# A software-pipelined attention and ternary kernel: the order of TensorE's steady step laid out anew

## What is computed

```python
q    = x + embed[stage][..., None]          # one value per row
attn = softmax(einsum('bsd,btd->bst', q, f))
y    = einsum('bst,btd->bsd', attn, f)
xh   = y @ H                                # 256x256 Hadamard
scale = clip(max|xh|, 1e-5) / 7
xq   = clip(round(xh / scale), -8, 7) * scale
wq   = ternary(weight)                      # -1, 0, 1 times a scale of each row
out  = x + einsum('bsi,oi->bso', xq, wq)
```

## Time and profile before

| | |
|---|---|
| three runs | 111.09, 111.1 and 112.66 us, median 111.1 |
| span of the profiled execution | 111.0 us (its own time lies within 0.1 us of the median, so little lies around the span) |
| busy share of the span | PE 93%, PEld 87%, DVE 80%, ACT 66%, POOL 39% |
| period of a steady step | 5.86 us, 12 steps |
| granted TensorE clock | full, except in the last two of the page's 40 slices (from 105.5 us), where it is half |

### The profile page before, as it was taken

One profiled execution on the slowest core, in us unless ns is written; L12 is line 12 of the kernel. 1 busy time (PEld: TensorE's weight loads), 2 busy tenths in 40 slices (PEclk: granted clock), 3 DMA queues, 4 the chain that ended last, 5 costly groups with the idle time before them and its releaser, 6 DMA issues.

```text
span 111.0 us, 2674 instructions
## 1 busy us (share of the span) xinstructions
PE 103.2 (93%) x853; PEld 96.2 (87%) x853; DVE 88.6 (80%) x217; ACT 73.5 (66%) x185; POOL 43.2 (39%) x50
## 2 busy tenths in 40 slices
PE   5999999999999999999999999999999999997360
PEld 2579899899999999999999999999999999996220
DVE  0165689799898988888898979797989898989681
ACT  5045885858787777777777778695878777494410
POOL 4025799304341461336243434343434031227150
PEclk9999999999999999999999999999999999999955
DMA  3986341405253352606161526252530202020214
GB/s 86 277 306 199 102 166 37 158 0 184 106 145 145 81 202 40 241 26 235 34 224 55 189 94 189 94 189 94 158 125 0 94 0 97 0 94 0 94 41 148
DMA packets 7630, 13.19 MB, mean 119 GB/s; under 512 B 834, under 2 KB 1608, under 8 KB 7624
## 3 DMA queue, kind: packets, MB, share of 16 engines
q1 hardware_dynamic: 7612, 13.12, 35.8%
q10 hardware_dynamic: 12, 0.00, 0.0%
HBM read 8.92 MB, written 4.19 MB: 118 GB/s over the span
## 4 chain that ended last, share of the span: by engine, by line
PE 84%; DVE 8%; ACT 3%; issue 2%
PE score_bank L415 18%; PE xh_bank L415 18%; PE fh_bank L415 14%; PE f_bank L404 6%; PE prob_bank L404 6%; PE out_bank L415 6%; PE q_bank L404 6%; PE out_bank L372 4%; PE code_bank L404 3%; DVE raw_scale L704 2%; DVE abs_max L697 1%; ACT prob L598 1%; PE score_bank L382 1%; ACT code L570 1%; DVE abs_max L822 1%
## 5 line engine op out<-in xcount | busy, mean ns | idle before, releaser
L304 POOL TENSOR_TENSOR result<-scaled,x_all 128x512 f32<-128x512 f32 x13 | 16.8, 1291 | 35.7 <-DVE scaled L714 35.7
L295 POOL TENSOR_TENSOR q_nat<-x_all,bias 128x512 f32 (+1 forms) x15 | 15.6, 1042 | 20.9 <-DMA x_all<-x_dram 15.2
L561 ACT CAST f_hi<-f_bank 128x512 fp32r<-128x512 f32 x16 | 9.4, 587 | 13.9 <-PE f_bank L404 13.9
L728 DVE TENSOR_TENSOR fh_lo<-fh_bank,fh_hi 128x512 fp32r<-128x512 f32 x16 | 11.0, 690 | 5.9 <-ACT fh_hi L592 5.9
L598 ACT ACTIVATE prob<-score_bank,neg_max 128x256 f32<-128x256 f32 x32 | 15.0, 479 | 0.8 <-DVE neg_max L755 0.8
L570 ACT ACTIVATE code<-xh_bank,inv_scale 128x256 f32<-128x256 f32 x30 | 12.8, 486 | 3.6 <-DVE inv_scale L709 3.6
L415 PE MATMUL fh_bank<-had,f_hi 128*128 128x256 f32 x64 | 14.4, 307 | 0.0
L415 PE MATMUL score_bank<-f_hi,q_hi 128*128 128x256 f32 x64 | 14.1, 301 | 0.0
L592 ACT CAST fh_hi<-fh_bank 128x512 fp32r<-128x512 f32 x16 | 9.4, 588 | 6.3 <-PE fh_bank L415 6.3
L415 PE MATMUL fh_bank<-had,f_lo 128*128 128x256 f32 x64 | 13.0, 284 | 0.0
L415 PE MATMUL score_bank<-f_lo,q_hi 128*128 128x256 f32 x64 | 12.9, 283 | 0.0
(11 more groups left out here) (99 smaller groups left out, 232.8 us busy)
## 6 DMA issues: line engine op xcount, KB each, us to landing
f_nat<-f_dram SPq DMA_DIRECT2D x16, 256.0 KB, 2.7
x_all<-x_dram SPq DMA_DIRECT2D x16, 256.0 KB, 2.8
out_dram<-result SPq DMA_DIRECT2D x14, 256.0 KB, 2.0
had_raw<-hadamard_dram SPq DMA_DIRECT2D x1, 256.0 KB, 3.2
w_raw<-weight_dram SPq DMA_DIRECT2D x1, 256.0 KB, 4.8
out_dram<-result SPq DMA_DIRECT2D x2, 128.0 KB, 1.7
out_dram<-scaled SPq DMA_DIRECT2D x1, 256.0 KB, 2.0
stage_of<-itok_dram ACTq DMA_DIRECT2D x1, 0.4 KB
```

The costliest lines, as they stand in the source:

```text
L295: nc.gpsimd.tensor_tensor(q_nat[:, b.k], x_all[:, b.at].rearrange("p (t d) -> p t d", t=T), bias[:, b.at].unsqueeze(2).broadcast_to([P, T, ...
L304: nc.gpsimd.tensor_tensor(result[:, b.k], as_rows(scaled[:, b.k]), x_all[:, b.at], ALU.add).then_inc(result_ready, 1)
L561: nc.scalar.copy(f_hi[:, b.k], f_bank[:, :, :]).then_inc(f_hi_ready, 1)
L728: return nc.vector.tensor_tensor(low, of[:, :, :], high.bitcast(F32), ALU.subtract)
```

## The change

Nothing is computed otherwise; the order is new. On PE a steady step is now written as three mixed blocks. `turns_with_score`: each of the four transposes of `prob` (batch i-2) stands ahead of one fp32r matmul of `score` (i-1), and eight more of these follow. `ternary_with_hadamard`: four fp32r matmuls of `times_hadamard`, the four code transposes (i-3), and then the four ternary matmuls, now of batch i-4 in place of i-3, each ahead of one of the other four Hadamard matmuls. `turns_with_mix`: the transposes of f and q, now of batch i+1 in place of i, each ahead of one of the first eight matmuls of `mix` (i-2); four more follow. ACT's list begins with `quantize` and ends with the splits of f and q of batch i+1; the exponentials come before `decode` and `split_fh`. DVE's list has `neg_max` directly behind `f_lo`, and `scaled` moves from behind `out_scale` to behind the sums. Step 3 is written out, with the transposes of batch 4 added and without a ternary product, and `times_ternary` of batch 12 stands ahead of the tail. POOL and SP are not touched.

```diff
+            def turns_with_score(b_prob, b_score):
+                wait(pe, prob_ready, b_prob.at + 1)
+                wait(pe, prob_lo_ready, b_prob.at)
+                wait(pe, f_lo_ready, b_score.at + 1)
+                wait(pe, q_lo_ready, b_score.at + 1)
+                wait(pe, prob_ready, b_score.at)
+                for n in range(6 * T):
+                    if n < C * T:
+                        turned = turn_one(prob_bank, prob, ident[:, :], n)
+                        if n == C * T - 1:
+                            turned.then_inc(prob_in_bank, 1)
+                    mm = product_one(score_bank, scored(b_score), n)
+                mm.then_inc(score_in_bank, 1)
+
+            def ternary_with_hadamard(b_code, b_out, b_fh):
+                parts = [(f_hi[:, b_fh.k], had), (f_lo[:, b_fh.k], had)]
+                wait(pe, f_lo_ready, b_fh.at + 1)
+                wait(pe, fh_lo_ready, b_fh.at)
+                for n in range(2 * C):
+                    mm = product_one(fh_bank, parts, n)
+                turn_code(b_code)
+                if b_out:
+                    wait(pe, code_t_ready, b_out.at + 1)
+                    wait(pe, scaled_ready, b_out.at)
+                for n in range(2 * C):
+                    if b_out:
+                        mm = product_one(out_bank, [(code_t[:, b_out.k], tern_t)], n)
+                        if n == T * C - 1:
+                            mm.then_inc(out_in_bank, 1)
+                    mm = product_one(fh_bank, parts, 2 * C + n)
+                mm.then_inc(fh_in_bank, 1)
+
+            def turns_with_mix(b_load, b_mix):
+                if b_load:
+                    wait(pe, f_loaded[b_load.k], 16 * b_load.half + 16)
+                    wait(pe, f_lo_ready, b_load.at)
+                wait(pe, prob_hi_ready, b_mix.at + 1)
+                wait(pe, fh_lo_ready, b_mix.at + 1)
+                wait(pe, code_ready, b_mix.at)
+                for n in range(6 * T):
+                    if n == 2 * C:
+                        if b_load:
+                            wait(pe, q_ready, b_load.at + 1)
+                            wait(pe, q_lo_ready, b_load.at)
+                        wait(pe, prob_lo_ready, b_mix.at + 1)
+                    if b_load and n < C * T:
+                        turned = turn_one(f_bank, f_nat[:, b_load.k], ident[:, :], n)
+                        ...
+                    elif b_load and n < 2 * C * T:
+                        turned = turn_one(q_bank, q_nat[:, b_load.k], ident[:, :], n - C * T)
+                        ...
+                    mm = product_one(xh_bank, mixed(b_mix), n)
+                mm.then_inc(xh_in_bank, 1)
             def step(batch):
...
+                turns_with_score(batch(LAG_MIX), batch(LAG_SCORE))
+                ternary_with_hadamard(batch(LAG_QUANT), batch(LAG_OUT), batch(LAG_SCORE))
+                turns_with_mix(batch(LAG_LOAD_TURN - 1), batch(LAG_MIX))
...
 # ACT
-                (split_f, LAG_LOAD_TURN), (split_q, LAG_LOAD_TURN), (quantize, LAG_QUANT),
-                (split_prob, LAG_MIX), (decode, LAG_QUANT), (split_fh, LAG_SCORE),
-                (exponentials, LAG_SCORE))
+                (quantize, LAG_QUANT), (split_prob, LAG_MIX), (exponentials, LAG_SCORE),
+                (decode, LAG_QUANT), (split_fh, LAG_SCORE),
+                (split_f, LAG_LOAD_TURN - 1), (split_q, LAG_LOAD_TURN - 1))
...
 # DVE
-                (scales, LAG_QUANT), (scale_out, LAG_OUT), (split_f, LAG_LOAD_TURN),
+                (scales, LAG_QUANT), (split_f, LAG_LOAD_TURN), (maximum, LAG_SCORE),
                 (split_q, LAG_LOAD_TURN), (split_prob, LAG_MIX), (sums, LAG_MIX),
-                (maximum, LAG_SCORE), (split_fh, LAG_SCORE))
+                (scale_out, LAG_OUT), (split_fh, LAG_SCORE))
```

More of the change, by code:

```diff
@@ L405, in turn, with turn_one, product_one @@
                 return mm
+            def turn_one(to, of, by, n):
+                c, t = divmod(n, T)
+                return pe.transpose(to[:, c, t * P:(t + 1) * P], of[:, t, c * P:(c + 1) * P], by)
+            def product_one(to, parts, n):
+                t, k = divmod(n, len(parts) * C)
+                (left, right), c = parts[k // C], k % C
+                return pe.matmul(to[:, t], left[:, c, t * P:(t + 1) * P], right[:, c],
+                                 start=k == 0, stop=k == len(parts) * C - 1)
             def product(to, parts, tiles=range(T), wait_for_last_part=None):
@@ L438, in score @@
                 wait(pe, prob_ready, b.at)
-                product(score_bank, [(q_hi[:, b.k], f_hi[:, b.k]), (q_hi[:, b.k], f_lo[:, b.k]),
-                                     (q_lo[:, b.k], f_hi[:, b.k])]).then_inc(score_in_bank, 1)
+                product(score_bank, scored(b)).then_inc(score_in_bank, 1)
             def low_half_words(of):
@@ L502, in _ @@
             mix(b0)
[L503 to L510, removed]
+            b3, b4 = Batch(0, 3), Batch(0, 4)
+            turn_f(b3)
+            turn_q(b3)
+            turn_prob(b1)
+            score(b2)
+            turn_code(b0)
+            weights()
+            times_hadamard(b2)
+            turn_f(b4)
+            turn_q(b4)
+            mix(b1)
+            pe.wait_ge(tern_t_ready, 1)
+            pe.wait_ge(row_ready, 1)
             for i in range(4, 2 * LOOP_FROM):
                 step(peeled(i))
-            with pe.Fori(LOOP_FROM, B // 2) as half:
+            with pe.Fori(LOOP_FROM, B // 2 - 1) as half:
                 for odd in range(2):
                     step(looped(half, odd))
-            third_last, second_last, last = (Batch(0, B - n) for n in (3, 2, 1))
+            for i in range(B - 2, B):
+                step(peeled(i))
+            fourth_last, third_last, second_last, last = (Batch(0, B - n) for n in (4, 3, 2, 1))
+            times_ternary(fourth_last)
             score(last)
@@ L611, in step @@
                         stage(b)
-            b0, b1, b2, b3 = (Batch(0, n) for n in range(4))
+            b0, b1, b2, b3, b4 = (Batch(0, n) for n in range(5))
             split_f(b0)
@@ L641, in _ @@
             decode(b0)
+            exponentials(b2)
             split_fh(b2)
-            exponentials(b2)
+            split_f(b4)
+            split_q(b4)
             for i in range(4, 2 * LOOP_FROM):
                 step(peeled(i))
-            with act.Fori(LOOP_FROM, B // 2) as half:
+            with act.Fori(LOOP_FROM, B // 2 - 1) as half:
                 for odd in range(2):
                     step(looped(half, odd))
+            for i in range(B - 2, B):
+                step(peeled(i))
             third_last, second_last, last = (Batch(0, B - n) for n in (3, 2, 1))
@@ L796, in _ @@
             split_q(b2)
[L797 to L801, removed]
+            b3 = Batch(0, 3)
+            scales(b0)
+            split_f(b3)
+            split_q(b3)
+            split_prob(b1)
+            sums(b1)
+            maximum(b2)
+            weight_copies()
+            split_fh(b2)
             for i in range(4, 2 * LOOP_FROM):
```

14 lines of the change are left out of this document (7 added, 7 removed).

## The result

The changed kernel takes 114.64 us (median of 4 executions, 114.23 to 114.94) against 111.3 us of the kernel before in the same series (111.09 to 112.66): ratio 1.029, 95% interval 1.025 to 1.033. In a second, longer series it was 1.019 (1.007 to 1.032). Their spans are 111.0 and 113.1 us, 2.1 apart. About 1.8 us of the time lies outside the span in every execution of which both are known (114.88 us for the span of 113.1).

What follows compares the result with a forecast made beforehand. PE's own instructions were taken to bound the kernel, 5.86 us a step. Ring steps, entry and step 3 sum to +2.1 us; against the median of 111.1 that gives 113.2 us, range 112.3 to 113.9, with rivals 110.6 to 115.0.

Steps and rivals of the forecast that it cites:

- The lock: On DVE, `raw_scale`, with two SBUF operands, waits until POOL's whole `q_nat` is over; predicted about 0.4 to 0.6 us.
- The ring: Loop of DVE and POOL alone through `q_nat`, `raw_scale`, `scaled`, `result`: period 6.07 us, total +2.1 us, 113.2; chance 0.60.
- Rival A: On DVE and POOL, the lock does not bite and `raw_scale` slips through: 111.0 us; chance 0.14.
- Rival C: On PE, changing kind costs up to 0.03 us at 16 places: 116.6 us, or 114.7 at 0.02; chance 0.16.
- PE's own sum: PE's instructions in a steady step after the change: 5.86 - 0.02 = 5.84 us.
- (c): On PE, a bf16 operand follows an fp32r matmul four times a step, not twice: about 0.01 each, +0.03 at most.
- (a): On PE, fp32r matmuls and transposes standing singly cost and bring nothing: 0, bounds -0.01 to +0.03 each.
- (b): At PE's code transposes, a ternary matmul with quickly loaded bf16 weights now stands behind: 0.29 falls to about 0.24, -0.05.
- the first shift of phase: One-time cost of entering the ring: about 0.1 us.
- step 3: Exponentials before `split_fh` on ACT make fh_lo of batch 2 later and push the first steady `abs_max`: 0.1 us.
- The tail: End of the run: the one moved ternary product only stands ahead of existing waits: 0, at most 0.2 us.

Runs made afterwards that it cites:

- `ternary_by_code`: Kernel before, with only the ternary matmuls (batch i-4) in one block directly behind the code transposes and `scaled` behind the maximum on DVE: ratio 1.007 (1.001 to 1.013).

## Why the prediction was right, and where it was not

**The lock and its place.** The mechanism was right: `q_nat` directly behind `result`, the wait for x gone from the steady steps, `raw_scale` ending with `q_nat` in ten steps, PEld waiting some 0.2 us for ACT's `code`. Only the size of the sign was off: `raw_scale` of 0.27 to 0.40 us, for the most part 0.35 to 0.38, where the text had 0.4 to 0.6. Two edits that leave POOL's work alone in amount (one moves it, one changes the operands' place) take the lengthening of `raw_scale` away.

**The ring.** Worked out as 6.07 us in POOL's loop; the six steps from 43.34 to 79.86 are 6.09. With one link of 0.13 out, it gave back 0.10; with PE made faster or later it didn't move. The eleven steady steps cost +1.99, where the prediction had 1.9 for ten of them. Of the cases, the ring (0.60) came in. Rival A is out, since the lock bites in every one of these steps. Rival C has the right sign, at 0.006 a change in place of 0.02 to 0.03.

**PE's own sum.** The wrong sign, and a small error. Predicted 5.84; with the ring gone the kernel runs at 5.88 in the steps where nothing waits. The term that failed most is (c), "about 0.01 each time, +0.03 at most": the four ternary matmuls between fp32r ones cost 0.242 a pair, 0.06 a step in all. Term (a), "standing singly costs and brings nothing", was nearly right at 0.003 or so a pair, 0.04 for twelve. Against them stands (b), the 0.05 at the code transposes: `ternary_by_code` has 0.24 from the first of them to the ternary matmul behind, and the whole step fell by 0.08, from 5.86 to 5.78. So 5.86 - 0.08 + 0.10 is 5.88. While the ring acts none of this shows.

**Steps 3 and 4.** The text had 0.1 for the first shift of phase and 0.1 for step 3. The entry is +0.98, but 0.87 of it is work that comes off the end again; 0.98 - 0.84 leaves 0.14.

**The tail.** "0, at most 0.2" was wrong by -0.4. The windows of both traces (length, then busy us and instructions of PE, PEld, DVE, ACT and POOL, then the granted clock) show the cause, first the kernel before, then the one after:

```profile
100.00:104.00 4.00, 2.33 (x21) 1.96 (x19) 3.78 (x8) 1.30 (x4) 2.55 (x2) 1.00 0.00 0
104.00:109.00 5.00, 2.34 (x12) 1.20 (x12) 3.13 (x9) 1.61 (x4) 1.41 (x2) 0.61 0.28 104
```

```profile
100.00:104.00 4.00, 4.00 (x36) 3.79 (x35) 3.35 (x10) 2.67 (x8) 1.47 (x2) 1.00 0.17 66
104.00:109.00 5.00, 2.28 (x20) 1.31 (x18) 4.01 (x12) 2.44 (x6) 1.94 (x3) 1.00 0.14 52
```

The granted clock fell to its lower level, 1.2 GHz, in the tail of the one and was still at 2.4 GHz over the same matmuls in the other. Two ternary matmuls take 0.61 to 0.64 us there before and 0.38 or 0.39 after. Up to the last batch's code transposes nothing differs: `abs_max` to these is 4.34 us before and 4.33 after. This gain and the +0.35 of the start (below) cancelled, so that the span of 113.1 us came out to the tenth for partly wrong reasons.

**The forecast of the time.** 113.2 against 114.64. That lies inside the whole range of 110.6 to 115.0, but outside the ring's own of 112.3 to 113.9; it is inside only because the range was widened for the milder half of rival C, which is not what happened. The step that failed is the last of the sum, "the profiled execution of 111.0 becomes 113.1; against the median of 111.1 the forecast is **113.2 us**". It took the span of 111.0 for an execution of 111.1 us, as the table of the kernel before does ("so little lies around the span"). With 1.8 us outside the span, as in every later execution, the profiled one took about 112.8 us and belongs with that of 112.66, and the same +2.1 on it gives 114.8 to 114.9, beside the 114.88 of the profiled execution after. The three times of before lay 1.6 us apart, and the nearness of two numbers was read as identity. The ratio of 1.029 is also made larger by this: three of its four executions of before lie at 111.1 to 111.5. The longer series has 1.019, which is 2.1 in 111.

## What to carry to other kernels

When a slot on one engine is freed or an order moved, list for every engine what now stands over what, and look for pairs of POOL with a DVE operation of two SBUF operands: the price is POOL's remaining time, however small the DVE operation. If that DVE operation also feeds POOL's next start, the two form a ring with a period of its own, which can be added up from rows of the trace and which no work on the busiest engine will shorten; ordering POOL behind it, or an operand in PSUM, breaks it. And before a sum is put on a median, settle which of the executions the trace is, by its span and what lies around it.

## What the runs showed of the hardware that was not expected

- A scalar_tensor_tensor of 128x2 with one input in PSUM takes 0.168 us, also in the thirteen of fifteen cases that started under a POOL operation, against 0.74 to 1.00 for the same with both in SBUF when POOL's operation has most of its time ahead.
- An fp32r matmul of 256 columns and a bf16 one in turn take 0.242 a pair; in blocks 0.118 and 0.109.
- Where PE's clock comes up differs between executions. The first four transposes of f took 1.11 us in both profiled runs of the kernel before, and 0.66 in that with the scales in PSUM (both rows below). The windows show a granted clock of 1.00 over both, but only because the trace has no clock record for the first microseconds. Its first record, of the full 2.4 GHz, begins at 9.53 us before and at 4.07 us with the scales in PSUM, and the matmuls become fast with it: two fp32r ones take 0.40 us from 9.57 on in the former. In twelve of the fourteen traces it begins at 9.1 to 10.4 us, in two at 3.8 and 4.1. The first `abs_max` with the scales in PSUM came at 16.42 in place of 17.81. That is 1.4 us, which is also what lies between the usual spans of the kernel before, 109.2 to 109.9 and 110.5 to 111.2 us; that the clock parts these is likely and was not shown. The +0.35 at the start has the same source: in the trace of after the record begins at 10.39 us, and two fp32r matmuls take 0.40 from 10.43 on.

```profile
5.24 1.11 PE L404 MATMUL f_bank<-ident,f_nat 128*128 128x128 f32 x4
```

```profile
4.78 0.66 PE L406 MATMUL f_bank<-ident,f_nat 128*128 128x128 f32 x4
```
